# The value projection of an attention and expert block: one plain float32 matmul per tile in place of three float32r passes

## What is computed

```python
h = layernorm(x) * (1 + ca) + sa
q, k, v = rotate(rot_w[0], h), rotate(rot_w[1], h), rotate(rot_w[2], h)   # 2x2 rotations of pairs
attn = softmax((2 + 2 * (q @ k.T)) / scale + bias)
ave = attn @ v
x = x + ga * ave / sqrt(clip(abs(sum(ave * ave))))
h = layernorm(x) * (1 + cb) + sb
# shared: (gelu(h @ Ws_g.T) * (h @ Ws_u.T)) @ Ws_d.T
# experts: the same form, on the top 64 rows of each sequence by softmax(h @ gate_w.T)
x = x + gb * (experts(h) + shared(h))
```

## Time and profile before

| | |
|---|---|
| median of 3 runs | 2466.16 us (2465.39 to 2470.37) |
| profiled execution | 2465.3 us, its span being the whole of it |
| PE busy | 2372.3 us, 96% of the span |
| PEld busy | 2086.3 us, 85% |
| DVE busy | 1567.9 us, 64% |
| POOL busy | 1150.4 us, 47% |
| ACT busy | 1032.8 us, 42% |
| V projection passes on PE | 768 (256 on each of lines 349, 350 and 351) |

### The profile page before, as it was taken

How to read it: one execution, slowest core, us unless ns; L and a number is a source line. 1 busy time by engine, 2 the same in 40 slices (tenths; PEclk the granted TensorE clock), 3 DMA queues, 4 the chain that set the end, 5 groups by cost and what they waited for, 6 DMA issues and landing times.

```text
span 2465.3 us, 40995 instructions
## 1 busy us (share of the span) xinstructions
PE 2372.3 (96%) x14388; PEld 2086.3 (85%) x14388; DVE 1567.9 (64%) x3198; ACT 1032.8 (42%) x1912; POOL 1150.4 (47%) x997
## 2 busy tenths in 40 slices
PE   6999999999998999999987999999999999999997
PEld 5888888888887888888876888888888888888886
DVE  6677767778776877788846455555554545555553
ACT  3545545444553545545442333333333333333332
POOL 1233333333332333333352666666666666666664
PEclk9999999999998999999998999999999999999999
DMA  2111111111111111111115444443444444434433
GB/s 90 53 44 59 51 60 60 52 51 57 54 61 44 60 43 60 52 60 60 59 62 90 86 90 82 88 84 66 79 84 87 86 85 88 84 60 86 84 62 43
DMA packets 78506, 167.03 MB, mean 68 GB/s; under 512 B 11744, under 2 KB 46720, under 8 KB 78368
## 3 DMA queue, kind: packets, MB, share of 16 engines
q0 software_dynamic: 49152, 67.14, 16.7%
q1 hardware_dynamic: 29216, 97.85, 11.8%
HBM read 97.71 MB, written 67.24 MB: 67 GB/s over the span
## 4 chain that ended last, share of the span: by engine, by line
PE 84%; DVE 6%; issue 4%; POOL 2%; DMA 1%; ACT 1%; SPq 0%; DVEq 0%; POOLq 0%; ACTq 0%
PE ps L349 26%; PE ps L351 26%; PE ps L350 26%; PE ps L501 2%; DVE stage L856 2%; PE ps L387 1%; DVE bn_stats L758 1%; PE ps L420 1%; DMA stage<-in_wd 1%; DVE x_t L753 1%; PE ps L442 1%; DVE hidden L753 1%; POOL rstd L1144 1%; POOL out L1209 1%; ACT x_t L693 0%
## 5 line engine op out<-in xcount | busy, mean ns | idle before, releaser
L349 PE MATMUL ps<-x_t,weights 128*128 128x512 f32 x1536 | 617.3, 402 | 23.2 <-DVE hidden_f L1111 13.3
L350 PE MATMUL ps<-x_t,weights 128*128 128x512 f32 x1536 | 602.5, 392 | 0.0
L351 PE MATMUL ps<-x_t,weights 128*128 128x512 f32 x1536 | 601.8, 392 | 0.0
L1209 POOL DMA_INDIRECT out<-x_rows,step_token x256 | 418.1, 1633 | 333.9 <-DVE x_rows L1090 275.4
L349 PE MATMUL ps<-weights,hidden 128*128 128x256 f32 x1536 | 435.8, 284 | 8.7 <-POOL hidden L1148 5.6
L351 PE MATMUL ps<-weights,hidden 128*128 128x256 f32 x1536 | 436.1, 284 | 0.0
L350 PE MATMUL ps<-weights,hidden 128*128 128x256 f32 x1536 | 436.0, 284 | 0.0
L1111 DVE TENSOR_TENSOR hidden_f<-gelu,ps 128x512 f32<-128x512 f32 x256 | 175.7, 686 | 379.0 <-ACT gelu L733 348.1
L733 ACT ACTIVATE gelu<-ps 128x512 f32<-128x512 f32 x256 | 152.8, 597 | 535.8 <-PE ps L351 508.4
L349 PEld LDWEIGHTS ps<-x_t,weights 128*128 128x128 f32 x1536 | 290.6, 189 | 83.6 <-DVE hidden_f L1111 13.5
L1148 POOL TENSOR_TENSOR hidden<-hidden_f,hidden 128x512 fp32r<-128x512 f32 x128 | 165.5, 1293 | 408.7 <-ACT hidden L647 408.7
(11 more groups left out here) (174 smaller groups left out, 4436.9 us busy)
## 6 DMA issues: line engine op xcount, KB each, us to landing
x_rows<-in_x SPq DMA_DIRECT2D x32, 512.0 KB, 3.5
pairs<-mod_rows SPq DMA_DIRECT2D x32, 512.0 KB, 4.3
h_rows<-stage SPq DMA_DIRECT2D x32, 512.0 KB, 2.6
out<-y_rows SPq DMA_DIRECT2D x32, 512.0 KB, 2.9
stage<-in_wg SPq DMA_DIRECT2D x16, 512.0 KB, 3.4
stage<-in_wd SPq DMA_DIRECT2D x16, 512.0 KB, 4.4
stage<-in_wu SPq DMA_DIRECT2D x16, 512.0 KB
x_rows<-h_rows,step_token POOLq DMA_INDIRECT x256
```

The costliest lines, as they stand in the source:

```text
L349: pe.matmul(o, lhs(HI), rhs(HI), start=start, stop=False)
L350: pe.matmul(o, lhs(HI), rhs(LO), start=False, stop=False)
L351: return pe.matmul(o, lhs(LO), rhs(HI), start=False, stop=stop)
L1209: pool.indirect_dma_start(out=out_rows, out_offset=bass.IndirectOffsetOnAxis(ap=ICUR[g][:, t:t + 1], axis=0), in_=X1[:, g % 2, t * D:(t + ...
```

## The change

The three passes of the V projection become one plain float32 matmul per tile, on `H1_F` and `ROTF[:, 1]`, the float32 values from which the halves were made. `ROTV` and the two DVE instructions that filled it at the start are gone. `H1_T` stays, since K and the scores read it. As PE now reads `H1_F`, SP waits for the last V projection as well before it loads expert weights over it.

```diff
-        ROTV = sb("rot_v", [P, 2, KD, P], F32R)
...
                     sp.wait_ge(xt_done, B)
                     sp.wait_ge(h1_lo, B)
+                    sp.wait_ge(v_done, B)
                     for m in (0, 2):
                         sp.dma_start(STAGE[:, m * WCOLS:(m + 1) * WCOLS], w_exp[m][0]).then_inc(w0_in, 16)
...
                 for t in range(T):
                     for k in range(KD):
-                        mm = mm3(PC[:, t * D + k * P:t * D + (k + 1) * P],
-                                 lambda a: H1_T[:, a, k, t * P:(t + 1) * P], lambda a: ROTV[:, a, k, :], True, True)
+                        mm = pe.matmul(PC[:, t * D + k * P:t * D + (k + 1) * P], H1_F[:, k, t * P:(t + 1) * P],
+                                       ROTF[:, 1, k, :], start=True, stop=True)
                 mm.then_inc(v_done, 1)
...
-                for m, (cc, ss, dst) in enumerate(((CS[:, 0, :], CS[:, 2, :], ROTK), (COS[:, 2, :], CS[:, 3, :], ROTV))):
+                for m, (cc, ss, dst) in enumerate(((CS[:, 0, :], CS[:, 2, :], ROTK), (COS[:, 2, :], CS[:, 3, :], None))):
...
-                    link(dve.tensor_copy(dst[:, HI, :, :], ROTF[:, m, :, :]))
-                    link(split_lo(dst[:, LO, :, :], ROTF[:, m, :, :], dst[:, HI, :, :]))
+                    if dst is not None:
+                        link(dve.tensor_copy(dst[:, HI, :, :], ROTF[:, m, :, :]))
+                        link(split_lo(dst[:, LO, :, :], ROTF[:, m, :, :], dst[:, HI, :, :]))
```

## The result

The changed kernel takes 2430.1 us (median of 5 executions, 2425.55 to 2431.34) against 2466.16 us. The medians differ by 36.1 us, the means of the executions by 38.8 us; the ratio of the two kernels is given as 0.9841, 95% interval 0.983 to 0.9853, which is 36 to 42 us less. A second set of executions gave 0.9848 (0.9834 to 0.9861). I had forecast 2439 us, 27 us less, in a range of 2430 to 2447 us. The median of 2430.1 us lies on the edge of that range, and 0.9841 of 2466.16 us, 2427 us, lies outside it. The direction was right; a quarter to a good third of the gain was missing from my sum.

The account below looks back on a forecast made before the run. PE was taken to bound the kernel; 31 x 0.79 = 24.5 us for the V stages, plus 1.6 at the low clock and 0.8 in the set-up, gave 26.9 us off: 2439 us, range 2430 to 2447.

Parts of the forecast that it names:

- What bounds the kernel: Whole kernel: PE, busy 2372.3 of 2465.3 us, bounds it; a microsecond of PE work removed comes off the end.
- Two loads and two passes for one plain matmul: V stage: each plain float32 matmul is two weight loads and two passes, so 16 passes replace 24.
- 0.115 us per pass: V stage: pace between 0.1115 (full overlap) and 0.1196 (attention times V); stage 1.84 against 2.63 us, 0.79 less per sequence.
- my bound of 0.92: V stage: largest saving per sequence in the forecast's bounds, 0.71 to 0.92 us around 0.79.
- The stage at the low clock: V stage of the one sequence at low clock: 5.01 us would become 3.4, 1.6 us less.
- No stall behind it: After the V stage: DVE's idle 0.90 us ahead of V's low part shrinks to about 0.1; scores don't wait.
- The set-up: Start of the kernel: DVE no longer splits the V rotation, so 0.79 us comes off once, on the path.
- SP's wait: Sequence 31: expert loads come less than 20 us later, the store of h2 not at all; cost nothing.
- The stops and the clock held as they were: Outer loop's turn near 746 us: the sum gave no change to PE's 5.23 us stop or the 17.0 us low clock.
- The rival: Stop near 746 us changes: without it 2426 us, with a second one 2452; chance 0.09 of over 5 us either way.
- the sign that I had set myself: Low-clock stretch near 750 us: another length there would show the prediction wrong.
- the two slower rivals: V stage: loads and passes don't overlap, +27 us, chance 0.05; four passes each with its own load, +29 us, chance 0.02.

Follow-up runs that it names:

- Experiment 5: Changed kernel with each plain matmul of V split in two of 64 columns on the same weights, 32 passes; 2494.99 us, ratio 1.0103.
- the repeats: Changed kernel run twice more without any edit, for its traces; 2429.22 us (ratio 0.9848) and, in a single execution, 2434.31 us.
- experiment 6: Changed kernel with the K projection in plain float32 too, 4 passes of 512 columns in place of 6 float32r passes; 2439.73 us, ratio 0.9883.
- experiment 7: Changed kernel with the two DVE instructions that make the V rotation's halves put back at the start, read by nobody; 2433.35 us in a single execution.

## Why the prediction was right and wrong

**What bounds the kernel**: right. PE's time counted one to one. Over 27 ordinary sequences (2 to 18 and 20 to 31) the kernel gained 24.7 us, 0.91 each, against 0.93 in the stage.

**Two loads and two passes for one plain matmul**: right, 16 passes per sequence.

**0.115 us per pass**: mis-sized. It was 0.1113, the full overlap, and I had taken a value between that and the pace of attention times V. Experiment 5 says why the lower neighbour was the right one: the pass is bound by its load, as the float32r pass of 128 columns is, and not by its columns. The rest is the stage's edge. The stage is 0.08 us shorter than 16 paces, which the earlier trace rows had shown for float32r as well (24 x 0.1115 = 2.68 against 2.63) and which I didn't carry over. So the stage lost 0.93 and not 0.79, above my bound of 0.92. Over 31 sequences that is 4.3 us too little.

**The stage at the low clock**: 3.15 us (3.04 and 3.06 in the repeats), not 3.4, so 1.86 less and not 1.6. The edge was missing here too, and the clock came back just before the stage's end.

**No stall behind it**: right, with little to spare. I had left DVE a tenth of a microsecond of idle time ahead of V's low part; 0.05 us are left between the end of K's split and that start, and 0.26 us between the end of V's low part and the scores. DVE's wait for ACT's copy of V came down to 3.1 us, where I had said some 7. What a larger shift would do was not run.

**The set-up**: 0.79 us on DVE, as forecast, not visible at the end. **SP's wait**: right. The loads are issued at 1178.89 us, right after the last V pass (1178.5), the store of h2 behind them at 1191.04, and ACT reads at 1237.64.

**The stops and the clock held as they were**: this is the step that failed. My sum put their change at nothing, and had it as a rival with a chance of 0.09. Outside the V stages and the set-up 6.0 us were gained. Of these 4.3 are at the turn, in three traces of three: PE's idle time there is 6.4 to 7.0 us before and 4.8 to 5.1 after, and the low clock lasts 6.8 us in place of 17.1. The 0.7 us at the start are within what chance does there. The rival had named the place, and its price of 2.3 us for a clock that is back right after the V stage is nearly what the clock gave (2.4). It priced the stop as a whole, but not the loss of the second one alone. I had it as an accident of code where it was a consequence of the change, and the sign that I had set myself, another length of that stretch, came true. These 6.0 us and the 4.6 of the mis-sized V stage (4.3 and 0.26) are the 10.6 us that my 26.9 lacked of 37.5.

All traces at the turn, in us. The last column is when the clock came back, counted from the end of the V stage.

| kernel | low clock starts ahead of the first K pass | second stop | low clock | clock back |
|---|---|---|---|---|
| before, 24 float32r (three traces) | 2.6 to 2.7 | 1.3 to 1.8 | 17.1 | 4.7 to 5.3 after |
| 24 plain | 2.6 | 1.5 | 10.2 | 0.9 ahead |
| 16 float32r | 1.9 | none | 10.2 | 2.4 after |
| 16 plain: changed (three traces) | 1.1 to 1.4 | none | 6.8 | 0.1 to 0.25 ahead |
| 16 plain: experiments 6 and 7 | 0.9 and 1.5 | none | 6.8 | 0.5 and 0.3 ahead |
| 32 plain of 64 columns | 1.2 | none | 13.7 | 3.1 after |

The first two rows differ in the kind of pass and in little else: the low clock starts at the same point, the second stop is there, and still it is 17.1 against 10.2 us. So what the V stage consists of counts, as far as one trace of the second kernel goes. What the number of passes does is not shown by itself, because with it the second stop and the start of the low clock change as well. Which property of the passes the clock answers to was not isolated. Only four lengths occur at the turn in the eleven traces, so that equal lengths say less than they seem to.

What stays open: why the second stop is there in both kernels with 24 passes and in none of the others; and the 1.4 us from sequence 31 to the end. There PE's wait for DVE's product at the start of phase B is 3 us shorter in the changed kernel (13.3 to 14.0 us before, 10.0 to 11.2 after), but experiment 7 has 14.1, so that this hangs on more than the change.

**The chances**: my 0.06 for slower is a point less than the two slower rivals together (0.07).

**The slower rivals** fall: loads and passes overlap, and there are not four loads. The Trainium skill (FP8 and Floating Point Precision, TensorE Precision Notes) has four passes for true FP32. For the columns the trace of experiment 6 agrees: two records of 0.43 us for 512 columns, 0.86 us, are about four times the 0.23 us of a float32r pass. At that width the plain form lost. At 128 columns the loads are what is paid for, and there are two.

## What to carry to other kernels

Count a stream of matmuls by weight loads and by columns, and take the larger: three float32r passes against one plain float32 matmul is three loads against two, and about one column time per pass against four in all. The plain form won at 128 moving columns (1.70 against 2.63 us) and lost at 512 (1.71 against 1.36). Where a trace has a stop with a low clock behind it, and the changed stage lies in that stretch, give the change of the stretch a price and a chance of its own: here it brought 4.3 us beyond the stage. Look at repeats of the trace before crediting a change with a gain in the start-up.

## What the runs showed of the hardware that I had not expected

- With 128 x 128 weights and 128 moving columns a plain float32 pass and a float32r pass have the same pace (0.1113 and 0.1115 us), and a plain pass keeps it with 64 columns (0.110).
- At the turn of the loop the low clock had the same length in each trace of a kernel (17.1 us three times, 6.8 us three times), while in the first 75 us the changed kernel had 7, 10 and 20 us of it.
- Writing out the outer loop removed a stop of 5 us in phase A, and in the same trace a loop of phase B had six more waits without a releaser, 4.9 us, which none of the six traces of the kernel before and of the changed kernel has.
